# The second part of a two-branch block: three pieces of work change their place in the turns of VectorE and ScalarE

## The reference, cut to what matters

```python
def attn_layer(x, Wqkv, qs, ksc, Wo):
    qkv = x @ Wqkv
    q, k, v = jnp.split(qkv, 3, -1)
    ...
    q = l2norm(q) * qs                # sums of squares over 64 numbers, root, product
    k = l2norm(k) * ksc
    ...
    q = q * cos * scale + rotate_half(q) * sin * scale
    k = k * cos * inv + rotate_half(k) * sin * inv
    out = local_attention(q, k, v)    # windows of 32 rows, each sees itself and the one before
    return out @ Wo
for i in range(DEPTH):                # 6
    x = attn_layer(shift_tokens(x), ...) + x
    x = ffn_layer(shift_tokens(x), ...) + x   # LayerNorm, 128 -> 2x341, a * gelu(gate), 341 -> 128
```

## Time and profile before

| what | before |
|---|---|
| median of 3 runs | 2050.93 us (2050.44 to 2051.26) |
| profiled execution | 2054.17 us, span of the core 2052.4 us |
| mean granted TensorE clock | 0.961 |
| busy: TensorE, VectorE, GpSimd, ScalarE | 1874.7, 1657.7, 1391.8, 1373.8 us |
| second part | from about 353 us to the end |

### The profile page before, as it was taken

The page is one execution under the profiler, slowest core; times in us unless marked ns, Lnnn a source line. Parts: engine busy times, 40 slices in busy tenths (PEclk is TensorE's granted clock), DMA queues, the critical chain, the costliest instruction groups (busy, mean ns, idle before and its releaser), DMA issues.

```text
span 2052.4 us, 74670 instructions
## 1 busy us (share of the span) xinstructions
PE 1874.7 (91%) x32776; PEld 1251.1 (61%) x32776; DVE 1657.7 (81%) x1819; ACT 1373.8 (67%) x2014; POOL 1391.8 (68%) x1277
## 2 busy tenths in 40 slices
PE   3999997889999999999899999999999999999985
PEld 1434443466666666666666666767666667677663
DVE  5777770889798888989888888799888888998852
ACT  1366565766777777777667776777677767777753
POOL 1011112999787889788877787878788878887810
PEclk7699999899999999999999999999999999999998
DMA  3041100232233323333233323233333333222221
GB/s 106 31 148 47 49 22 23 55 88 68 69 86 77 91 68 86 89 78 87 65 84 71 98 65 91 65 88 86 78 86 73 83 90 76 68 69 66 70 66 47
DMA packets 144036, 151.52 MB, mean 74 GB/s; under 512 B 60760, under 2 KB 85596, under 8 KB 142944
## 3 DMA queue, kind: packets, MB, share of 16 engines
q1 hardware_dynamic: 143712, 146.75, 28.5%
HBM read 35.75 MB, written 5.44 MB: 20 GB/s over the span
## 4 chain that ended last, share of the span: by engine, by line
PE 39%; DVE 22%; SPq 15%; issue 10%; ACT 9%; DMA 3%; POOL 1%; DVEq 0%; ACTq 0%; POOLq 0%
SPq L1314 12%; PE banks L485 6%; PE banks L579 4%; DVE arena L643 3%; PE banks L422 3%; PE banks L512 3%; PE banks L525 3%; DVE ss L732 3%; DVE arena L781 3%; DVE mx_t L767 3%; PE banks L494 3%; PE banks L552 3%; PE banks L589 3%; PE banks L562 2%; DVE arena L740 2%
## 5 line engine op out<-in xcount | busy, mean ns | idle before, releaser
L1150 POOL TENSOR_TENSOR arena<-arena,tab_sl 128x512 f32<-128x512 f32 x384 | 589.9, 1567 | 15.8 <-ACT arena L951 8.3
L1158 POOL TENSOR_TENSOR arena<-arena 128x1024 f32<-128x1024 f32 x192 | 491.9, 2582 | 0.0
L485 PE MATMUL banks<-w_qkv,arena 128*128 128x512 f32 x768 | 370.0, 627 | 30.9 <-ACT arena L932 24.7
L740 DVE TENSOR_TENSOR arena<-arena,rn 128x1024 f32<-128x1024 f32 x192 | 374.6, 1991 | 5.4 <-POOL rn L1129 5.0
L982 ACT ACTIVATE arena<-arena 128x1024 f32<-128x1024 f32 x96 | 101.5, 1058 | 354.6 <-DVE arena L771 354.6
L485 PEld LDWEIGHTS banks<-w_qkv,arena 128*128 128x128 f32 x768 | 144.0, 197 | 189.4 <-issue 180.1
L781 DVE TENSOR_TENSOR arena<-banks,tab_cl 128x1024 f32<-128x1024 f32 x192 | 226.6, 1219 | 26.1 <-ACT arena L951 24.3
L643 DVE TENSOR_REDUCE arena<-banks 128x1 f32<-128x512 f32 (+3 forms) x352 | 183.4, 587 | 66.3 <-PE banks L382 57.2
L889 ACT ACTIVATE arena<-banks 128x512 f32<-128x512 f32 (+2 forms) x352 | 156.4, 529 | 100.3 <-PE banks L404 89.8
L1100 POOL TENSOR_SCALAR_AFFINE_SELECT arena<-arena 128x512 f32<-128x512 f32 x64 | 40.9, 640 | 267.5 <-ACT arena L889 267.3
L732 DVE TENSOR_REDUCE ss<-arena 128x32 f32<-128x2048 f32 x96 | 218.5, 2276 | 1.3 <-ACT arena L957 1.3
(11 more groups left out here) (111 smaller groups left out, 3021.2 us busy)
## 6 DMA issues: line engine op xcount, KB each, us to landing
arena<-arena SPq DMA_DIRECT2D x1512, 64.0 KB, 2.0
arena<-parts_dram SPq DMA_DIRECT2D x64, 144.0 KB
w_qkv<-Wqkv SPq DMA_DIRECT2D x6, 1024.0 KB, 5.5
parts_dram<-arena SPq DMA_DIRECT2D x12, 256.0 KB, 3.0
tab_cl<-tab_c SPq DMA_DIRECT2D x6, 512.0 KB, 7.2
tab_sl<-tab_s SPq DMA_DIRECT2D x6, 512.0 KB
w_o<-Wo SPq DMA_DIRECT2D x6, 512.0 KB
w_qkv<-Wqkv SPq DMA_DIRECT2D x6, 512.0 KB, 4.3
```

Of the source, the lines that this page charges most:

```text
L485: last = e.matmul(ps[:, BANK * c:BANK * (c + 1)], xsT[b][:, P * t:P * (t + 1)], w_qkv[:, at:at + BANK], start=True, stop=True)
L740: e.tensor_tensor(to, to, rn[n % 4][:, HEADS * m:HEADS * (m + 1)].unsqueeze(2).to_broadcast([P, HEADS, HEAD_DIM]), ALU.mult).then_inc(S["r ...
L1150: e.tensor_tensor(qk_sw[:, m, :].rearrange("p (h d) -> p h d", d=HEAD_DIM)[:, :, d:d + HALF], raw[:, m, :].rearrange("p (h d) -> p h d", d ...
L1158: e.tensor_tensor(to, to, qk_sw[:, m, :], ALU.add).then_inc(S["rs"], 1)
```

## The change

Three pieces move. On VectorE `norms(s-1)` goes from ahead of `rotate(s)` to behind `normalise(s-4)`. On ScalarE `project` is cut in two: the two copies stay near the start, the first now ahead of the exponentials and the second behind them (in steps with k = 2 both ahead), and roots and squares become a function of their own, `squares`, which stands at the end of the turn, behind `weights` and `shift_in` and ahead of the Gelu. What is computed, and the number of instructions, stay the same.

```diff
@@ vector_program, loop over s
-                if 0 <= s - 1 < n_tiles:
-                    norms(s - 1)
                 if s < n_tiles:
                     rotate(s)
...
                     sums(s - 4)
                     normalise(s - 4)
+                if 0 <= s - 1 < n_tiles:
+                    norms(s - 1)
@@ scalar_program
-            def project(n):
-                raw = qk_raw[n % 2]
-                for m in range(2):
-                    w.wait_ge(S["proj"], 2 * n + m + 1)
-                    if n >= 2:
-                        w.wait_ge(S["sw"], 4 * (n - 1))
-                    e.copy(raw[:, m, :], banks[:, pair_of["proj", n, m], :]).then_inc(S["raw"], 1)
+            def project(n, m):
+                w.wait_ge(S["proj"], 2 * n + m + 1)
+                if n >= 2:
+                    w.wait_ge(S["sw"], 4 * (n - 1))
+                e.copy(qk_raw[n % 2][:, m, :], banks[:, pair_of["proj", n, m], :]).then_inc(S["raw"], 1)
+
+            def squares(n):
                 w.wait_ge(S["ss_sum"], n)
                 if n:
                     roots(n - 1)
                 for m in range(2):
                     w.wait_ge(S["raw"], 2 * n + m + 1)
...
+                if s < n_tiles:
+                    project(s, 0)
+                if s < n_tiles and s >= FF and k == 2:
+                    project(s, 1)
                 if 0 <= s - 4 < n_tiles:
                     exponents(s - 4)
-                if s < n_tiles:
-                    project(s)
-                if s == n_tiles:
-                    roots(s - 1)
+                if s < n_tiles and not (s >= FF and k == 2):
+                    project(s, 1)
...
                     shift_in((s + 1) // GROUP)
+                if s < n_tiles:
+                    squares(s)
+                if s == n_tiles:
+                    roots(s - 1)
                 if ff_here and k == 3:
                     ff_gelu(G)
```

More of the change, by code:

```diff
@@ L956, in project @@
                     w.wait_ge(S["raw"], 2 * n + m + 1)
-                    e.activation(qk_sq[:, m, :], raw[:, m, :], ACT.Square).then_inc(S["sq"], 1)
+                    e.activation(qk_sq[:, m, :], qk_raw[n % 2][:, m, :], ACT.Square).then_inc(S["sq"], 1)
             def turn(n):
```

## The result

The changed kernel takes 2041.62 us, median of 5 runs (2034.37 to 2045.96), against 2050.93 before, beside it (2047.76 to 2051.26): ratio 0.9949 [0.993, 0.9968], 9.3 us faster. The forecast was 2016, that is 35 us faster. The direction was right and the time lies in the range, but the gain is a quarter of what was foreseen. The profiled execution has a span of 2039.8 us, 12.6 less than before, at the same granted clock (0.962 against 0.961).

What follows compares the result with a forecast made beforehand. TensorE was taken to set the pace. A quiet group (not held by late V copies) gains -2.8 + 0.45 + 0.4 = -1.95 us; thirteen give -25, eight others -8, first steps and tail -2: -35, so 2016 us, range 1994 to 2046.

Steps and rivals of the forecast that it cites:

- (1): VectorE's sums of squares behind the normalisation: rotary product starts 2.3 us earlier, line 494's wait goes; B -1.6 us, A -0.3.
- B: Second step of a group of four (k = 2), counted from TensorE's projection start; forecast from 15.69 to 14.09 us before (5).
- (5): Cost coming back in B: normalisation meets GpSimd's line 1158, ends at 11.65 us while TensorE wants it at 11.2; +0.45 us.
- A: First step of a group of four (k = 1), 14.80 us in an undisturbed group; forecast -0.3 us.
- (4): Line 740's scaling meets GpSimd's Newton instructions instead of line 1150; VectorE gains 1.6 us in B, 1.6 in C, about 1.0 in A.
- (2): Roots and squares at the end of ScalarE's turn: the wait for line 992's copy in C goes, -0.9 us.
- C: Third step of a group of four (k = 3), holding the Gelu; forecast from 20.24 to 19.33 us.
- (6): Squares before the Gelu in C delay the first gate to 19.25 us, so D may start late: +0.4 us (bounds 0 and 1.5).
- D: Fourth step of a group of four (k = 0), 16.41 us in an undisturbed group; its projection waits for the gates.
- slower rival: Squares in front of the Gelu end 18.9 us or later into C, cancelling the -2.8 us; 2071 us at worst costed; chance 0.11.
- SyncE's queue: Rival: window copies and loads on SyncE take over as bound, line 978 waiting for DMA far above 25.9 us; 2028; chance 0.16.
- The lag only moves: Rival: VectorE still enters B 3.4 us late or more, line 552 waiting for line 771; -0.5 us a group, 2041; chance 0.15.

## Why the prediction was right, and where it failed

**Right: (1).** The product comes before the sums of squares and the waits of line 494 go: 14.8 us in 13 waits before, 2.1 in 10 after. B fell by 1.12 in the mean; the forecast for a quiet group was -1.6 + 0.45 = -1.15. That the two agree is partly luck: in the median B fell by 1.48, and the 0.45 of (5) hardly came. A fell by 0.87 in the mean, where 0.3 was put down. The turn of VectorE in A was added up wrongly in (4): 17.3 less 1.0 and plus 0.25 is 16.55 us, not 16.8. It took 16.22 (1858.12 to 1874.34), and VectorE enters B 2.0 us late instead of the 2.4 said.

**Right: (4), the size of line 740.** Said "near 1.6 us instead of 2.0"; it is 1.31. But this term was carried through VectorE only.

**Right about its own wait, wrong about the step: (2). This is the step that failed.** The wait of line 525 for line 992 goes, as said. C was to fall by 0.9 us, to 19.33, and rose by 0.74 in the mean. The forecast had 1.6 us a group in all (33 us over 21), measured were 0.61; the error in C, 0.9 booked as gain in quiet groups and 0.74 lost, is larger than the whole miss of 1.0, and A gave some of it back. Two things were wrong in it.

The first is the three C with a late V copy, 11.8 of the 15.5 us. The groups held back by V copies were given half a gain, -1 each. That a V copy which waits for its DMA stands ahead of squares, table load and Gelu on ScalarE, and so comes out of the room that (6) had just used up, has no term in the sum. In step 29 the squares end 21.6 us into C and TensorE waits 2.53 us for the first gate. Both edits that take away one side of it, loads spread and squares behind the Gelu, bring these steps to 20.5 to 21.1 us.

The second is the ordinary C, which did not fall at all. In the group shown VectorE enters C 1.4 us late, even less than the 1.9 foreseen, and from there on two terms went wrong. GpSimd's small instructions of the inverse deviation were nowhere in the sum: its rotation starts 8 to 10 us later in all four steps, since the roots come at the end of ScalarE's turn (in A behind the shift copies too), and so the deviation, which stands behind the rotation, falls beside line 740. ScalarE's first copy in C starts 4.5 us into it; by the prediction's own working (2.15 + 1.68) it starts at 3.8. And the lock at the normalisation in C was sized 0.25 us; it was 1.0 (2.25 instead of 1.25). Together they bring the normalisation's end from the foreseen 11.05 us into C to 12.5, and the first gate's end from 19.25 to 20.4. The Trainium skill (SBUF — State Buffer, "SBUF: two separate sides") says that a VectorE instruction with two inputs in SBUF and a GpSimd one that reads SBUF take the shared port by turns, each for the whole of itself. The rows agree for small instructions too (1.06 us for one that took 0.23 before), and what was wrong was my reading of who meets whom.

**Right in kind, too small: (6).** D lost 0.63 in the mean (0.50 in the pair without large GpSimd products; medians 0.62 and 0.76), where 0.4 was said with bounds 0 and 1.5. With C in the old order D is back at 16.49; with the squares alone behind the Gelu at 16.81. The slower rival named the same mechanism. Its point of decision, squares that end 18.9 us into C, is passed in step 29, but through the late V copy and not through VectorE.

**Right in kind, too large: (5) in B.** The normalisation beside the sums takes 2.63 us there (+1.4), but TensorE waits for it only 3.2 us over all 21 B, 0.15 us a group instead of 0.45. It was looked for in a single place, though, and line 760 meets line 1164 in A (2.08) and C (2.25) as well; over the 21 C TensorE waits 10.4 us for it.

**The rivals.** SyncE's queue: the sign it named appeared (line 978 waits 42.0 us instead of 25.9), and its price shows in three C, through one layer's loads each; a whole group held by the queue did not come, and nor did its time, 2028. *The lag only moves*: its time, 2041, is what was measured, but that is luck, since its sign is missing (line 552 does not wait for line 771 beyond 0.6 us); line 740 does meet other instructions than 1150. I gave it 0.15, because I had costed one meeting of the two engines at a time.

**Open** is how the rest of C's loss, 0.2 us a step where 0.9 was to be gained, splits between the late inverse deviation, the normalisation beside line 1164 and what ScalarE brings late into C. Each was taken away once, and each time the meeting of VectorE and GpSimd moved with it. Open is also why the V copies wait for their DMA more often (23 waits instead of 14): spreading the loads takes most of it away, but what shifted in SyncE's queue was not followed. A run with the squares behind the Gelu and the deviation first was not made, nor one with the squares behind the Gelu and the loads spread.

## What to carry to other kernels

When an edit takes a wait away, follow every engine's timetable through the whole period, the third engine's too: here GpSimd's rotation came 8 to 10 us later in every step, since the roots that it waits for had moved to the end of ScalarE's turn. Ask too what stands ahead of the moved work in bad steps: the squares fitted in front of the Gelu as long as the V copy ahead of them was not late. Look at the single steps behind a mean; three of 21 made most of what C lost. Where two engines hold each other up, an order is worth what its meetings are worth, and those shift with every further edit, so that gains of single edits do not add; try them in combination before building on one. And an edit whose two halves only work together (2605 and 2066 us apart, 2042 together) is best costed from the wait that each half creates for the other.

## What the runs showed of the hardware

A tiny GpSimd instruction can lose as much as a large one when it meets VectorE. The 128x4 instructions of the inverse deviation take 0.22 and 0.23 us in the kernel before and 1.09 and 1.06 beside line 740, close to the length of one of VectorE's (1.2). VectorE's product of line 781, which reads one of its two inputs from PSUM (`banks`), is not held up: its pair at 1876.72 takes 2.35 us beside line 1156 (1875.64 to 1879.94), and its mean over the whole run is 1.22 us.

And it goes both ways: VectorE's normalisation, 1.22 us alone, takes 2.08 to 3.17 beside GpSimd's sums, and the pair of line 740 has been seen at 2.35, 4.17, 4.51 and 5.54 us. Cutting GpSimd's large products to one head of sixteen, with the order of before, made the whole kernel 1.65% faster, more than any order that was tried.

Between ScalarE's table load (1903.95, 1.28 us) and the Gelu (1905.24) lie 0.01 us, though squares that end at 1903.93 stand directly ahead. What the Trainium skill adds to a load (ScalarE: Activation LUTs, "What ACT_TABLE_LOAD costs": a drain of 1.38 us) does not show here either, in this new place.
